# An AdaLN block on one core: setup, last pair, output path and the order of all steps are rewritten

## What is computed

```python
mod = (silu(c) @ wmod).reshape(16, 6, 1, 256)
sa, ca, ga, sb, cb, gb = (mod[:, i] for i in range(6))
ga, gb = (sign(g) * maximum(abs(g), 0.25) for g in (ga, gb))
h = layernorm(x) * (1 + ca) + sa
q, k, v = h @ Wq.T + bq, h @ Wk.T + bk, h @ Wv.T + bv
w = softmax(where(causal, abs(q @ k.T / 16), -inf))
x = x + ga * ((w @ v) @ Wo.T + bo)
h = layernorm(x) * (1 + cb) + sb
# FFN: cluster = argmax over 8 of calibrate(h @ cluster_signatures.T)
#      tile = argmax over the cluster's 8 of calibrate(h @ signatures.T)
#      comp = tanh(gelu(h @ w1 + b1) @ w2 + b2)
#      mag = relu(comp @ spline_w1[tile] + spline_b1[tile]) @ spline_w2[tile] + spline_b2[tile]
y = h + mag * directions[tile] * output_scale
x = x + gb * (layernorm(y) * norm_gamma + norm_beta)
```

## Time and profile before

| what | value |
|---|---|
| median of 3 runs | 471.96 us (468.45 to 473.19) |
| the profiled execution | 471.67 us |
| its span | 469.8 us, mean granted TensorE clock 0.931 |
| busy PE / VectorE / ScalarE / GpSimd | 399.8 / 398.5 / 296.5 / 67.4 us |
| DMA | 28.72 MB, mean 61 GB/s |

### The profile page before, as it was taken

One profiled execution on the slowest core, in us unless ns is written; L12 is line 12 of the kernel. 1 busy time (PEld: TensorE's weight loads), 2 busy tenths in 40 slices (PEclk: granted clock), 3 DMA queues, 4 the chain that ended last, 5 costly groups with the idle time before them and its releaser, 6 DMA issues.

```text
span 469.8 us, 7656 instructions
## 1 busy us (share of the span) xinstructions
PE 399.8 (85%) x2072; PEld 308.7 (66%) x2072; DVE 398.5 (85%) x1367; ACT 296.5 (63%) x645; POOL 67.4 (14%) x82
## 2 busy tenths in 40 slices
PE   2697899999999999899989998999899999463330
PEld 2555578777777877687768776877677778452220
DVE  4417637387859899999999999999999899999996
ACT  2230365877698769676967697769776976651400
POOL 1002310302020002400250015001400220031040
PEclk9977899999999999999999999999999999796565
DMA  8503102101200213112310231122100210040112
GB/s 292 142 30 105 74 23 79 35 1 45 69 23 1 69 45 114 45 28 86 114 45 25 91 112 47 22 91 86 50 1 1 73 64 1 4 130 0 35 57 89
DMA packets 26234, 28.72 MB, mean 61 GB/s; under 512 B 3888, under 2 KB 21552, under 8 KB 26192
## 3 DMA queue, kind: packets, MB, share of 16 engines
q1 hardware_dynamic: 24160, 26.38, 17.8%
q10 hardware_dynamic: 2032, 1.85, 1.2%
HBM read 19.77 MB, written 8.45 MB: 60 GB/s over the span
## 4 chain that ended last, share of the span: by engine, by line
DVE 45%; PE 42%; issue 8%; ACTq 2%; ACT 2%; DVEq 0%
PE bank L511 8%; PE bank L530 8%; PE bank L490 6%; PE bank L500 6%; PE bank L553 3%; DVE y L1278 3%; DVE y L1246 3%; DVE x L1091 3%; DVE res L1288 3%; DVE st L1254 2%; DVE probs L1077 2%; DVE st L1046 2%; PE bank L520 2%; ACTq L680 2%; DVE v L1070 2%
## 5 line engine op out<-in xcount | busy, mean ns | idle before, releaser
L511 PE MATMUL bank<-h,g 128*128 128x128 f32 (+3 forms) x256 | 80.2, 444 | 4.9 <-DVE v L1070 4.9
L978 POOL TENSOR_TENSOR res<-x,gb_row 128x512 f32<-128x512 f32 x32 | 44.5, 1407 | 268.3 <-DMA out<-res 268.3
L530 PE MATMUL bank<-v,probsT 128*128 128x257 f32 x320 | 79.1, 382 | 0.0
L500 PE MATMUL bank<-m_ga,h 128*128 128x258 f32 x256 | 68.8, 394 | 5.2 <-DVE rows L1360 3.2
L530 PEld LDWEIGHTS bank<-v,probsT 128*128 128x128 f32 x320 | 57.1, 190 | 6.6 <-DVE y L1246 0.3
L490 PE MATMUL bank<-h,a_sb 128*128 128x512 f32 x128 | 60.4, 595 | 0.0
L511 PEld LDWEIGHTS bank<-h,g 128*128 128x128 f32 x256 | 44.7, 195 | 22.1 <-issue 8.5
L500 PEld LDWEIGHTS bank<-m_ga,h 128*128 128x128 f32 x256 | 47.7, 197 | 15.7 <-issue 4.3
L736 ACT ACTIVATE bank<-bank,v 128x128 f32<-128x128 f32 (+1 forms) x64 | 31.7, 495 | 41.4 <-PE bank L511 29.1
L1077 DVE CUSTOM_DVE_ANT_0 probs<-bank,cmask 128x128 f32<-128x128 f32 (+1 forms) x64 | 31.1, 485 | 23.3 <-ACT bank L736 23.3
L742 ACT ACTIVATE probs<-probs,negmax 128x128 f32<-128x128 f32 (+1 forms) x64 | 35.5, 557 | 5.9 <-DVE negmax L1077 5.9
(11 more groups left out here) (167 smaller groups left out, 770.1 us busy)
## 6 DMA issues: line engine op xcount, KB each, us to landing
x<-in_L_attn_x SPq DMA_DIRECT2D x16, 512.0 KB, 3.5
out<-res SPq DMA_DIRECT2D x16, 512.0 KB, 3.0
a_row<-gate_rows SPq DMA_DIRECT2D x16, 256.0 KB, 3.2
gb_row<-gate_rows SPq DMA_DIRECT2D x16, 256.0 KB, 3.2
wide<-in_L_wmod ACTq DMA_DIRECT2D x2, 768.0 KB, 7.6
res<-in_L_attn_Wq SPq DMA_DIRECT2D x1, 256.0 KB, 5.0
res<-in_L_attn_Wk SPq DMA_DIRECT2D x1, 256.0 KB, 7.3
res<-in_L_attn_Wo SPq DMA_DIRECT2D x1, 256.0 KB, 10.1
```

Of the source, the lines that this page charges most:

```text
L500: last = mm(ps[:, 0:VW], h[s][:, c, t * P:(t + 1) * P], m_ga[p % 2][s][:, c, :], start=(c == 0), stop=(c == KC - 1))
L511: last = mm(ps[:, 0:w], g[s][:, c, t * P:(t + 1) * P], h[s][:, c, 0:w], start=(c == 0), stop=(c == KC - 1))
L530: last = mm(ps[:, 0:D + 1], probsT[s][t][:, j * P:(j + 1) * P], v_sb[s][:, j, 0:D + 1], start=(j == 0), stop=(j == t))
L978: gp.tensor_tensor(res[:, 2 * u:2 * u + 2, :], x2[p % 2][s][:, t, :], gb_row[p % 2][s][:, 1:2, :].broadcast_to([P, 2, D]), ALU.add).then_i ...
```

## The change

1. *Setup*: silu is taken after the turn of `c` (on 128x32 and not 16x256). `A`, `woT` and the turned signatures are evicted by ScalarE, two of the four first `xhat` tiles and one `h` by VectorE. The signature columns and the table (`sp_sig`, `sp_rest`) are made by GpSimd, ahead of its first `ms`. Gate rows of sequences 0 and 1 are made by products that spread them at once (`su_gax`, `sd_gax`, `sd_gab`) and don't go through DRAM. Constants are loaded by SP, the attention biases by GpSimd's queue.
2. *Last pair*: the FFN works on groups, `GROUPS` = the pairs 0 to 6, then sequence 14 and sequence 15 each alone (4 tiles). Attention still goes by pairs.
3. *Output*: for the groups of pairs 0 to 6 ScalarE normalises `y` (`yh`, one instruction a tile), GpSimd multiplies by the gate row (`yg`) and adds into `res` (`yo`), two tiles an instruction. Groups 7 and 8 keep `oa` and `ob`.
4. *Orders*: no superstep; each engine's steps are written out for the whole run, so that the mix differs from pair to pair. `BANK` is new too. The Chains' counts are plain running counts.

The diff, cut to its core:

```diff
+        GROUPS = [(2 * p, 2 * p + 1) for p in range(PAIRS - 1)] + [(B - 2,), (B - 1,)]
+        BY_DVE = PAIRS - 1
...
+            def yh(g, t):
+                act.wait_ge(ln3_ready, g + 1)
+                A(y[:, t, :], y[:, t, :], ACT.Identity, bias=ln3["nmr"][:, t:t + 1],
+                  scale=ln3["rstd"][:, t:t + 1]).then_inc(yhat_rdy, 1)
...
+            def yg(g, u):
+                pool.wait_ge(yhat_rdy, NT * before(g) + 2 * u + 2)
+                pool.wait_ge(gb_ld[g % 2][u // 2], 16 * gb_uses(g, u // 2))
+                own = y[:, 2 * u:2 * u + 2, :]
+                tt(own, own, gb_row[g % 2][u // 2][:, 0:1, :].broadcast_to([P, 2, D]), ALU.mult).then_inc(scaled_rdy, 1)
+            def yo(g, u):
+                pool.wait_ge(scaled_rdy, 2 * before(g) + u + 1)
+                pool.wait_ge(base_rdy, 2 * before(g) + u + 1)
+                own = res[:, 2 * u:2 * u + 2, :]
+                tt(own, own, y[:, 2 * u:2 * u + 2, :], ALU.add).then_inc(res_rdy, 2)
...
+            def sp_sig():
+                pool.wait_ge(sig_rdy, 1)
...
+            def sp_rest():
+                pool.wait_ge(temp_rdy, 1)
...
+                link(ts(table[:, :], t_full[:, :], 1.0, None, ALU.mult))
+                link(tt(t_full[lo, :], t_full[lo, :], table[lo, :].bitcast(F32), ALU.subtract))
+                ts(table[lo, :], t_full[lo, :], 1.0, None, ALU.mult).then_inc(ffn_rdy, 1)
...
             def ms(p, s):
                 if seq(p, s) == 0:
                     pool.wait_ge(m_rdy, 1)
+                if p == 0:
+                    pool.wait_ge(ga_own[s], 1)
...
             def b_v(p, s, t):
                 b = seq(p, s)
                 dve.wait_ge(v_done, NT * b + t + 1)
                 if t == 0:
+                    if p == 0:
+                        dve.wait_ge(ga_first[s], 1)
...
+            def sd_gax(b):
+                dve.wait_ge(ga_two[b], 1)
+                gate_rows_of(ga_raw, ga_sign, a_row[0][b][:, 0:D], banks[BANK[f"su_gax{b}"]][:, 0:D]).then_inc(ga_own[b], 1)
+            def sd_gab(b):
...
+                tt(a_row[0][b][:, D:2 * D], vb_bc[:, 0:D], a_row[0][b][:, 0:D], ALU.mult).then_inc(ga_first[b], 1)
+            def sd_rest():
+                dve.wait_ge(in_rest, 16 * 14)
```

More of the change, by code:

```diff
@@ L675, in _ @@
+            for i in range(0, 2):
+                BT(8, i)
         @block.scalar
@@ new lines, in _ @@
+            a_xh(2, 1, 2)
+            b_abs(1, 0, 1)
+            b_exp(1, 0, 0)
+            a_xh(2, 1, 3)
+            b_abs(1, 0, 2)
+            b_exp(1, 0, 1)
+            b_abs(1, 0, 3)
+            b_exp(1, 0, 2)
+            b_pt(1, 0, 0)
+            gelu(0)
+            b_abs(1, 1, 0)
+            for i in range(1, 3):
+                b_pt(1, 0, i)
+            a_h(2, 0, 0)
+            tanh(0)
+            b_exp(1, 0, 3)
+            elo(0)
+            b_exp(1, 1, 0)
+            b_abs(1, 1, 1)
@@ new lines, in _ @@
+            a_nw(3, 0)
+            y_nw(0, 3)
+            for i in range(1, 4):
+                a_nw(3, i)
+            for i in range(0, 10):
+                clc(1, i)
+            b_v(2, 1, 2)
+            c_b2(1)
+            for i in range(10, 12):
+                clc(1, i)
+            for i in range(0, 4):
+                clb(1, i)
+            b_ttr(2, 0, 0)
+            clb(1, 4)
+            b_ttr(2, 0, 1)
+            for i in range(0, 2):
+                pick(1, i)
+            for i in range(0, 2):
+                loc(1, i)
@@ new lines, in _ @@
+            a_nw(4, 0)
+            y_nw(1, 3)
+            for i in range(1, 3):
+                a_nw(4, i)
+            b_v(3, 1, 1)
+            clc(2, 0)
+            a_nw(4, 3)
+            for i in range(1, 12):
+                clc(2, i)
+            for i in range(0, 5):
+                clb(2, i)
+            b_ttr(3, 0, 0)
+            pick(2, 0)
+            c_b2(2)
+            pick(2, 1)
+            for i in range(1, 3):
+                b_ttr(3, 0, i)
+            for i in range(0, 2):
+                loc(2, i)
@@ new lines, in _ @@
+            b_v(4, 1, 0)
+            clc(3, 0)
+            a_nw(5, 3)
+            clc(3, 1)
+            b_v(4, 1, 1)
+            for i in range(2, 12):
+                clc(3, i)
+            clb(3, 0)
+            b_ttr(4, 0, 0)
+            for i in range(1, 4):
+                clb(3, i)
+            c_b2(3)
+            b_ttr(4, 0, 1)
+            clb(3, 4)
+            for i in range(0, 2):
+                pick(3, i)
+            for i in range(0, 2):
+                loc(3, i)
+            for i in range(2, 4):
+                b_ttr(4, 0, i)
@@ new lines, in _ @@
+            clc(7, 11)
+            clb(7, 0)
+            c_b2(7)
+            for i in range(1, 5):
+                clb(7, i)
+            for i in range(0, 2):
+                pick(7, i)
+            for i in range(0, 5):
+                spl(6, i)
+            c_nw(8, 0)
+            spl(6, 5)
+            loc(7, 0)
+            y_(6, 0)
+            loc(7, 1)
+            c_nw(8, 1)
+            loc(7, 2)
+            c_nw(8, 2)
+            loc(7, 3)
+            c_nw(8, 3)
+            loc(7, 4)
@@ new lines, in _ @@
+            clb(8, 0)
+            y_nw(6, 2)
+            clb(8, 1)
+            y_nw(6, 3)
+            for i in range(2, 4):
+                clb(8, i)
+            spl(7, 0)
+            clb(8, 4)
+            spl(7, 1)
+            pick(8, 0)
+            spl(7, 2)
+            pick(8, 1)
+            for i in range(3, 5):
+                spl(7, i)
+            loc(8, 0)
+            spl(7, 5)
+            for i in range(1, 10):
+                loc(8, i)
+            y_(7, 0)
+            loc(8, 10)
```

3243 lines of the change are left out of this document (2433 added, 810 removed), and 16 rows, old and new, of the table BANK.

## The result

| | before | after |
|---|---|---|
| median | 471.62 us (468.45 to 473.19) | 506.38 us (505.88 to 507.59) |
| ratio | | 1.075, 95% interval 1.069 to 1.081 |
| span of the profiled execution | 469.8 us | 504.1 us |
| mean granted TensorE clock | 0.931 | 0.917 |
| the last `b_x2` of pair 0 starts at | 79.1 us | 63.8 us |

The setup gave 15.3 us, the end 4.5, and the middle took 54 (pair 1 4.5, the others 49.6).

The account below looks back on a forecast made before the run. VectorE was taken to bound the steady pairs (busy 47.30 of 47.51 us), TensorE close at 46.0. 36.2 + 29.8 + 44.2 + 278.4 = 388.6, plus 56.0 for the end: 444.6 us span, 1.9 around it, say 446; range 431 to 464.

Parts of the forecast that it names:

- setup and pair 0: Start through pair 0: V(0,0,0) at 34 us, 36.2 us to where 49.82 stood, then 29.8 us as before.
- pair 1: Second pair: 42.2 us as before plus 2 us of GA, 44.2 us.
- six steady pairs: Middle of the run: six pairs at 46.4 us, 278.4 us; the step falls from 47.5 to 46.4.
- the end: After the last `x2` statistics of pair 7: from 67.4 us to 56.0, bounds 52 to 61.
- Rival C: Setup doesn't shorten: `ms(0,0)` waits behind SP's loads, V at 39 us or more; 451 to 456 us; with D 0.13.
- The price of a GpSimd operation: Steady pairs: VectorE's loss s for each GpSimd operation, taken as 0.70 us, bounds nothing and 1.29.
- the pair costs 36.6 + 14 s: Steady pair: VectorE's own 36.6 us plus loss s for each of 14 GpSimd operations; 46.4 us at s 0.70.
- the 6.3 us off VectorE: Steady pairs: `oa` and `ob` removed, 16 instructions of about 0.40 us a pair; step to fall only from 47.5 to 46.4.
- Rival A: Steady pairs: `yg`, `yo` stretch `clc` and `clb`, PE waits; at s = 0.9 49.2 us a pair, 463 us; chance 0.22.
- The Trainium skill's rule: VectorE and GpSimd instructions on SBUF block each other whole; at full length a pair of 54.6 us, span some 494.
- D: Steady pairs, ScalarE: eight `yh` before gelu and `b_abs`, late by 1 us a pair; 452 us; with Rival C 0.13.

Follow-up runs that it names:

- e6: New setup with the old orders, groups and output (e4), but the changed kernel's PSUM banks for setup and pair 0: 460.81 us, ratio 0.980.
- e14: e6 with all but the first `base` of a pair, and `ms`, waiting on GpSimd until the routing's `pick` is done: 450.38 us, ratio 0.959.
- e2: Changed kernel with `yg` and `yo` on 8 of 256 channels, every instruction and wait kept: 463.33 us, ratio 0.986.
- e16: Changed kernel with `yg` whole and only `yo` on 8 of 256 channels: 484.48 us, ratio 1.030.
- e1: Changed kernel with all output by `oa` and `ob` on VectorE, no `yh`, `yg`, `yo`: 498.92 us, ratio 1.061.
- e4: New setup and new order of pair 0, with the orders, banks, eight pairs and VectorE output of the kernel before: 465.60 us, ratio 0.988.
- e17: Changed kernel with `yh`, `yg` and `yo` all on 8 of 256 channels: 464.72 us, ratio 0.985.
- run 30: Not a follow-up run: words of "PE has run 30 products more", a count of PE's products up to pair 7's mark; no kernel or time belongs to it.
- e7: Changed kernel with `yg` and `yo` waiting until `onehot` of the next group is made, SP's loads of `x` moved ahead: 487.15 us, ratio 1.032.
- e18: New setup, old orders, output by `yh`, `yg`, `yo`, all three on 8 of 256 channels: 469.50 us, ratio 0.996.

## Why the prediction was wrong

The sum was 444.6 us of span, measured were 504.1. By its own terms (its stages end about half a us behind the marks):

| term | predicted | measured | difference |
|---|---|---|---|
| setup and pair 0 | 36.2 + 29.8 = 66.0 | 63.8 | -2.2 |
| pair 1 | 44.2 | 46.6 | +2.4 |
| six steady pairs | 6 x 46.4 = 278.4 | 330.4 | +52.0 |
| the end | 56.0 | 63.3 | +7.3 |

- **Setup: right.** V started at 32.87 where 34 stood, and e6 and e14 keep the gain with other orders. Rival C did not come.
- **The price of a GpSimd operation: nearly right.** 0.70 us was taken; the share of VectorE's busy time above 36.6 us a pair is (48.3 - 36.6) / 14 = 0.84, which makes +1.9 us a pair. And e2, e16 and the changed kernel give 0.76 to 0.78 of span for each added one. In the six steps e2 takes 0.71 us off VectorE for each of 48 operations, and its short ones still last 0.22 us of 1.27.
- **The step that failed: "the pair costs 36.6 + 14 s".** It took over from the earlier trace rows that VectorE is full, and so let a pair last as long as VectorE is busy. That fullness belonged to the superstep, which was being replaced. With the written-out orders VectorE waits 6.7 us a pair (6.2 in e2, without the port's time, and for the same inputs), and 48.3 + 6.7 is the step of 55.1 but for rounding. Six times 1.9 and 6.7 are the 52 us. Neither bound of the term had a place for it: the floor was TensorE's 46, and VectorE's share could only take its place. So the waits were put at nothing. That they come with the new orders is shown (e1, with these orders, their banks and groups, is 33 us longer than e4 with the same output); which part of them does it is open.
- **What became of the 6.3 us off VectorE.** They are in the step of neither e2 nor e17, where the port costs next to nothing: 48.8 and 49.1, over the old orders' 46.8 with 2.3 us more work on VectorE. Some is work moved forward: up to pair 7's mark PE has run 30 products more than before in pairs 1 to 7 (236 + 1491 against 217 + 1480), some 5.5 us at the 0.184 us that one takes in the steady pair of the earlier trace rows, of which 2 were counted. The rest is about 10 us of idle PE in e2. Its trace puts 3.5 us of them to `b_ttr` and 3.5 to `oh`; no run moved either.
- **Rival A was the case, mis-priced.** Place and mechanism are in the trace as it said them (`b_ttr` behind `clc`, PE waiting). But it was priced by the same sum, s = 0.9 for 463 us and s = 1.0 for no change, so 0.84 looked harmless. It should have had the stall's consequences: an idle PE, then score products at the lower clock. From 0.99 (e2) to 0.95 are some 26 us more at 1.2 GHz (an estimate from the clock and length of the six steps in the two kernels), worth up to half of that.
- **The Trainium skill's rule (SBUF — State Buffer, Who interferes with whom), taken at full length for each operation, gave 494 us** and so came nearer than the sum, for a part of the reason. In the chain shown above the trace agrees with it: one short step to each operation of 1.26 us. Over a whole pair it took 0.84 of VectorE's time and not 1.29, since not every operation meets such a step: e7 ran `yg` and `yo` beside `b_x2` and `b_st`, and in its second and third step VectorE was no busier than with short ones. The rest of the measured step was waiting.
- **D: no.** `yh` short changed nothing in the new orders (e17), as the prediction's cover said; in the old ones it was worth 10 us (e18).
- **The end.** GpSimd has 12 operations in it, and the four above the 8 of before were put at 3 us. With its eight `yg` and `yo` short VectorE is busy 45.7 us in it (e2) and not 53.1, and the end is 58.0: 5.3 of the 7.3 us.

That the time lay above the range follows from one omission: the sum had no engine waiting in the middle. A named PE's wait and gave it no price, and D priced ScalarE's at 1 us a pair.

## What to carry to other kernels

When an order is replaced, the fullness of the bounding engine is not a property that is kept: price a stage as its busy time plus its waits, and give the waits a range of their own, with the row of what each engine would wait for. Before work goes to GpSimd, list the short instructions of VectorE on SBUF alone that will run beside it (the elementwise steps of a routing, a variance, a Newton step) and what stands behind them; beside PSUM reads and `bn_stats` the same operation cost nothing here (e7), and a wait that moves what is already there may bring more than new work there. PSUM banks belong to an order: the old ones under the new setup put pair 0's mark 12 us later, and 4.8 us of that stood in the median.

## What was new about the hardware

- Back to back, GpSimd's 128x512 operations let one VectorE instruction through each: steps of 128x64 that take 0.20 to 0.22 us took 1.11 to 1.22 in the changed kernel, and 1.18 to 1.30 in e6 beside `base` and `ms`. `b_x2` (0.48 us), reciprocals from PSUM (0.16) and `bn_stats` (0.43) took no longer beside them in e7.
- One idle stretch of TensorE in the middle of a run is paid twice. After 5.43 us without a matmul the mean granted clock was 0.64 from 253.1 to 262.7, and twelve score products took 6.22 us, where e2 runs these twelve and four more in 4.56; with an idle stretch of 3.39 us in e6 the step's clock was 0.97. The kernels with full steps (e14) hold 1.00.
